# Causal attention on one core: fp32r pieces with two heads in 64-row tiles, row maxima folded per 512 queries in a stream ahead of the scores, PV two steps behind

## What is computed

```python
def attn(x, W_qkv, b_qkv, W_proj, b_proj):          # H = 16, HS = 16
    q, k, v = split(heads(x @ W_qkv + b_qkv))
    q, k = rope(q), rope(k)
    att = einsum('bhqd,bhkd->bhqk', q, k) / sqrt(HS)
    att = softmax(where(causal, att, -1e9), axis=-1)
    return merge(einsum('bhqk,bhkd->bhqd', att, v)) @ W_proj + b_proj
x = layernorm(x + attn(x))
x = layernorm(x + moe_ffn(x))
```

## Time and profile before

| | |
|---|---|
| median of three runs | 1558.74 us |
| profiled execution | 1565.56 us |
| its span | 1563.8 us |
| PE busy, share of the span | 1339.1 us, 86% |
| DVE | 1167.3 us, 75% |
| ACT | 799.7 us, 51% |
| POOL | 276.2 us, 18% |
| DMA moved | 126.96 MB, mean 81 GB/s |

### The profile page before, as it was taken

How to read it: one execution, slowest core, us unless ns; L and a number is a source line. 1 busy time by engine, 2 the same in 40 slices (tenths; PEclk the granted TensorE clock), 3 DMA queues, 4 the chain that set the end, 5 groups by cost and what they waited for, 6 DMA issues and landing times. The chain is left out here.

```text
span 1563.8 us, 26808 instructions
## 1 busy us (share of the span) xinstructions
PE 1339.1 (86%) x7840; PEld 655.1 (42%) x7840; DVE 1167.3 (75%) x2833; ACT 799.7 (51%) x1130; POOL 276.2 (18%) x282
## 2 busy tenths in 40 slices
PE   6766299899999998998998998999947765999997
PEld 3433111233333233332332332332236655999997
DVE  6997499898897797986996896880036754888886
ACT  3443100366665565665665665668825443545452
POOL 3554500001001001011001001011123331121112
PEclk9887555799999999999998999999978876999999
DMA  4587592001201201102112113000045623333420
GB/s 163 174 192 228 155 140 36 2 29 29 82 29 54 58 29 56 55 28 79 33 50 79 29 37 83 8 9 14 14 149 167 214 78 98 101 100 114 137 95 23
DMA packets 117980, 126.96 MB, mean 81 GB/s; under 512 B 14428, under 2 KB 100447, under 8 KB 117856
## 3 DMA queue, kind: packets, MB, share of 16 engines
q1 hardware_dynamic: 114272, 116.97, 26.4%
q0 software_dynamic: 3584, 8.47, 1.5%
HBM read 82.98 MB, written 48.38 MB: 84 GB/s over the span
## 5 line engine op out<-in xcount | busy, mean ns | idle before, releaser
L622 ACT ACTIVATE probs<-scores 128x1024 f32<-128x1024 f32 (+3 forms) x640 | 540.7, 895 | 415.7 <-PE scores L524 414.8
L669 DVE TENSOR_REDUCE part_max<-ring 128x1 f32<-128x512 f32 x768 | 484.5, 685 | 34.1 <-PE ring L552 32.2
L552 PE MATMUL ring<-k_stack,q_stack 96*128 96x512 bf16 (+3 forms) x1280 | 433.8, 383 | 64.7 <-DMA k_stack<-pieces_d 29.9
L524 PE MATMUL scores<-q_stack,k_stack 99*128 99x512 bf16 (+3 forms) x1280 | 344.1, 358 | 12.4 <-ACT probs L622 6.3
L542 PE MATMUL out_p<-probs,v_s 128*32 128x512 f32 (+3 forms) x2560 | 306.9, 552 | 9.3 <-POOL probs L714 5.5
L664 DVE CUSTOM_DVE_ANT_0 scratch<-ring,mask_s 128x384 f32<-128x384 f32 (+3 forms) x512 | 229.6, 488 | 100.9 <-issue 88.2
L552 PEld LDWEIGHTS ring<-k_stack,q_stack 96*128 96x128 bf16 x1280 | 120.5, 99 | 418.0 <-DVE part_max L669 170.3
L714 POOL TENSOR_SCALAR_AFFINE_SELECT probs<-probs 128x512 f32<-128x512 f32 x128 | 81.2, 634 | 865.6 <-ACT probs L622 865.6
L524 PEld LDWEIGHTS scores<-q_stack,k_stack 99*128 99x128 bf16 x1280 | 114.0, 100 | 169.9 <-ACT probs L622 67.6
L195 PE MATMUL psP<-xT,wqk_s 128*128 128x512 f32 x128 | 72.4, 731 | 34.5 <-ACT xT L234 30.7
L542 PEld LDWEIGHTS out_p<-probs,v_s 128*32 128x32 f32 x2560 | 51.6, 109 | 112.4 <-issue 90.5
(11 more groups left out here) (116 smaller groups left out, 1455.6 us busy)
## 6 DMA issues: line engine op xcount, KB each, us to landing
w_whole<-w SPq DMA_DIRECT2D x16, 1024.0 KB, 6.3
q_stack<-pieces_d SPq DMA_DIRECT2D x192, 64.0 KB, 2.7
k_stack<-pieces_d SPq DMA_DIRECT2D x192, 64.0 KB, 2.8
v_d<-vt SPq DMA_DIRECT2D x8, 1024.0 KB, 4.4
v_s<-v_d SPq DMA_DIRECT2D x8, 1024.0 KB, 6.0
o_d<-o_s SPq DMA_DIRECT2D x32, 256.0 KB, 2.1
p_o<-o_d SPq DMA_DIRECT2D x8, 1024.0 KB, 6.0
slots_d<-no_row SPq DMA_DIRECT2D x1, 5200.0 KB, 30.3
```

The costliest lines, as they stand in the source:

```text
L524: last = nc.tensor.matmul(scores[p][:, hh, off:CHUNK], k_stack[i][0:KROWS, j, kb * P:(kb + 1) * P], q_stack[i][0:KROWS, j, c * CHUNK + off ...
L552: nc.tensor.matmul(ring[m % 3][:, 0:w], q_stack[i][0:SROWS, j, qt * P:(qt + 1) * P], k_stack[i][0:SROWS, j, t * CHUNK:t * CHUNK + w], star ...
L622: nc.scalar.activation(probs[n % 2][:, 2 * p:2 * p + 2, off:CHUNK], scores[p][:, :, off:CHUNK], ACT.Exp, scale=SCALE).then_inc(exp_done[p], 1)
L669: nc.vector.tensor_reduce(out, ring[m % 3][:, 0:w], axis=AX.X, op=ALU.max).then_inc(ring_read, 1)
```

## The change

- **Pieces.** `TERMS` has three products instead of six, over two pieces (`hi`, `low`) of type fp32r (stored as 4 bytes). `rest`, `cut_mid` and the tile `mid` are gone; `low` is raw minus hi on GpSimd. A stack is 48 rows and 2 rows of the maximum: 50 rows, so one head lies in rows 0 to 63 and another in rows 64 to 127.
- **Scores.** The two matmuls of a pair p use the two halves of the rows. Each writes its own PSUM bank.
- **Maxima.** 144 blocks per unit (`ITEMS`): a full block is one head, 48 rows; diagonal blocks of 128 and 256 columns hold two heads of one row half. In each diagonal block TensorE adds the causal mask by a further bf16 matmul of 128 columns (identity times mask) to each head, and VectorE always uses `tensor_reduce`. The blocks go by chunk of queries, and there are three folds per unit (chunk 3, chunk 2, chunks 1 and 0), each with its transpose, its cut (`cut_maxima`) and 4 DMAs (`load_max`). The stream runs 74 items (`LEAD`) ahead of the scores and on over the units without a break; only these 74 are done ahead of the first score.
- **PV** lags two steps (`LAG`), `probs` has four buffers, and the PV of a step is issued in two halves of 256 columns, one behind each pair of scores.
- The rows of ones come by DMA instead of a memset on GpSimd; unit 1's stacks are loaded after the first maxima.

```diff
-TERMS = [(0, 0), (0, 1), (1, 0), (1, 1), (0, 2), (2, 0)]
+TERMS = [(0, 0), (0, 1), (1, 0)]
...
-NPIECE = 3
+NPIECE = 2
...
-        hi = [sb(f"hi{i}", [P, QKG, CHUNK], BF16) for i in range(2)]
-        mid = [sb(f"mid{i}", [P, QKG, CHUNK], BF16) for i in range(2)]
-        low = [sb(f"low{i}", [P, QKG, CHUNK], BF16) for i in range(2)]
+        hi = [sb(f"hi{i}", [P, QKG, CHUNK], F32R) for i in range(2)]
+        low = [sb(f"low{i}", [P, QKG, CHUNK], F32R) for i in range(2)]
...
-            def cut_mid(b, c, g):
-                i, n = c % 2, NCH * b + c
-                act.wait_ge(rest_ready, QKG * n + g + 1)
-                nc.scalar.activation(mid[i][:, g, :], rots[i][:, g, :], ACT.Copy).then_inc(mid_ready, 1)
...
+NPROB = 4
+LAG = 2
+def max_items():
+    items, fold_after, turn_at = [], {}, {}
+    for c in ORDER:
+        block = []
+        for t in range(c, -1, -1):
+            for qt in range(TPC * c, TPC * (c + 1)):
+                w = (qt + 1) * P - t * CHUNK if t == c else CHUNK
+                if 2 * w <= CHUNK:
+                    block += [(qt, t, half, 2, w, True) for half in range(2)]
+                else:
+                    block += [(qt, t, j, 1, w, t == c) for j in range(HPU)]
+        before = {NCH - 1: 2, NCH - 2: 0, NCH - 3: 1}.get(c)
+        if before is not None:
+            block.insert(3, before)
+            turn_at[before] = len(items) + 3
+        items += block
...
+LEAD = TURN_AT[0] + 10
...
+            def score_pair(u, i, n, p):
+                c, kb, off = STEPS[n]
+                pe.wait_ge(exp_done[p], NSTEP * u + n)
+                for hh in range(2):
+                    rows = slice(hh * HALF, hh * HALF + KROWS)
+                    last = nc.tensor.matmul(scores[p][:, hh, off:CHUNK],
+                                            k_stack[i][rows, kb // TPC, p, kb % TPC * P:(kb % TPC + 1) * P],
+                                            q_stack[i][rows, c, p, off:CHUNK],
+                                            start=True, stop=True)
+                last.then_inc(scores_ready[p], 1)
...
+            def max_item(u, i, m, uses):
+                qt, t, j, heads, w, diag = ITEMS[m]
...
+                    pe.wait_ge(ring_read, NRING * u + m - 2)
+                slot = ring[m % 3][:, 0:heads * w]
+                for h in range(heads):
+                    rows = slice(j % 2 * HALF, j % 2 * HALF + SROWS)
+                    pair = j // 2 if heads == 1 else h
+                    last = nc.tensor.matmul(slot[:, h * w:(h + 1) * w], ...
+                                            start=True, stop=not diag)
+                    if diag:
+                        last = nc.tensor.matmul(slot[:, h * w + w - P:(h + 1) * w], id16[:], mask_s[:],
+                                                start=False, stop=True)
+                last.then_inc(ring_full, 1)
...
+            def step(u, i, uses, n, ahead, behind):
+                first, stop = PLAN[n]
+                middle = (first + stop) // 2
+                chunk_waits(u, n)
+                score_pair(u, i, n, 0)
+                items(u, i, uses, first, middle, ahead)
+                if behind:
+                    pv_waits(*behind[0:1], behind[2])
+                    pv_cols(behind[1], behind[2], FIRST_COLS)
+                score_pair(u, i, n, 1)
+                items(u, i, uses, middle, stop, ahead)
+                if behind:
+                    pv_cols(behind[1], behind[2], LAST_COLS)
...
             def read_max(u, m):
-                    nc.vector.tensor_tensor_reduce(out=scratch[:, j, 0:w], in0=ring[m % 3][:, 0:w],
-                                                   in1=mask_s[:, CHUNK - w:CHUNK], scale=1.0, scalar=LOWEST,
-                                                   op0=ALU.add, op1=ALU.max, accum_out=out).then_inc(ring_read, 1)
...
+                    nc.vector.tensor_reduce(part_max[:, qt, j:HPU:2, t],
+                                            ring[m % 3][:, 0:heads * w].rearrange("p (h w) -> p h w", h=heads),
+                                            axis=AX.X, op=ALU.max).then_inc(ring_read, 1)
```

More of the change, by code:

```diff
@@ L382, in max_plan @@
+ITEMS, FOLD_AFTER, TURN_AT = max_items()
+NRING = len(ITEMS)
+FOLDS = [(NCH - 1,), (NCH - 2,), tuple(range(NCH - 3, -1, -1))]
+FOLD_OF = [2, 2, 1, 0]
+NMAXROW = [HPU * TPC * len(f) for f in FOLDS]
+assert NRING % 3 == 0
+LEAD = TURN_AT[0] + 10
+def max_plan():
+    cost = [0.6 if isinstance(item, int) else 0.08 + item[3] * item[4] / 960 for item in ITEMS]
+    width = [CHUNK - off for _, _, off in STEPS]
+    plan, m, seen, done = [], LEAD, 0, 0.0
+    for w in width:
         seen += w
         start = m
-        while m < NMAX and sum(jobs[:m + 1]) - early <= seen / total * (sum(jobs) - early) + 1e-6:
+        while m < LEAD + NRING and done + cost[m % NRING] <= seen / sum(width) * sum(cost) + 1e-6:
+            done += cost[m % NRING]
@@ L385, in max_plan, with attention @@
             m += 1
-        plan[n] = range(start, m)
-    assert m == NMAX
+        plan.append((start, m))
+    assert m == LEAD + NRING
     return plan
 PLAN = max_plan()
[L393 to L398, removed]
+def attention(nc, pieces_d, v_d, causal16, ident, ident16, o_d):
@@ L476, in store_o, with unit @@
                 sp.dma_start(o_d[NCH * b + c, g], o_s[c % 2][:]).then_inc(o_stored[c % 2], 16)
[L478 to L483, removed]
+            def unit(u, b, g, i, last, two_ahead):
+                load_max(1, i, NRING * u + TURN_AT[1] + 1)
+                store_o(u, b, g, 3)
+                if two_ahead:
+                    load_chunk(two_ahead[0], two_ahead[1], i, 3)
+                load_max(2, i, NRING * (u + 1) + (1 if last else TURN_AT[2] + 1))
+                store_o(u, b, g, 2)
+                if two_ahead:
+                    load_chunk(two_ahead[0], two_ahead[1], i, 2)
+                if not last:
+                    load_max(0, 1 - i, NRING * (u + 1) + TURN_AT[0] + 1)
+                for c in (1, 0):
@@ new lines, in max_item, with turn_maxima, maxima @@
+                last.then_inc(ring_full, 1)
+            def turn_maxima(f, u, m):
+                pe.wait_ge(folded[f], u + 1)
+                pe.wait_ge(ring_read, NRING * u + m - 2)
+                nc.tensor.transpose(ring[m % 3][0:NMAXROW[f], 0:P], row_max[f][:], id_s[:]).then_inc(ring_full, 1)
+            def maxima(u, i, uses, first, stop):
+                for m in range(first, stop):
+                    if isinstance(ITEMS[m], int):
+                        turn_maxima(ITEMS[m], u, m)
+                    else:
+                        max_item(u, i, m, uses)
@@ new lines, in items, with chunk_waits @@
+            def items(u, i, uses, first, stop, ahead):
+                maxima(u, i, uses[0], min(first, NRING), min(stop, NRING))
+                if stop <= NRING:
+                    return
+                if ahead:
+                    maxima(u + 1, 1 - i, uses[1], max(first, NRING) - NRING, max(stop, NRING) - NRING)
+                elif first <= NRING:
+                    turn_maxima(2, u + 1, 0)
+            def chunk_waits(u, n):
+                c, kb, _ = STEPS[n]
+                if kb == 0 and c != 0:
+                    f = FOLD_OF[c]
+                    pe.wait_ge(max_loaded[f], MAX_PRIMED[f] + MAX_DMAS * (u + 1))
```

365 lines of the change are left out of this document (163 added, 202 removed).

## The result

The change makes the kernel slower: 2035.6 us (median of four runs, 2018.47 to 2037.93) against 1558.58 (four runs), a ratio of 1.304, 95% interval 1.3004 to 1.3077. The forecast was 1462, its range ended at 1570, and the slower rival stood at 1597.

What follows compares the result with a forecast made beforehand. PE was taken to bound the units, DVE close behind. Projection 10, lead 44 and units 42 us made 96 off the profiled 1565.6 us: 1470, or 1462 against the median; range 1365 to 1570.

Steps and rivals of the forecast that it cites:

- the slower rival: Scores: fp32r matmuls of two row halves run one behind the other, 121 us a unit, 1597 us in all; chance 0.13.
- Projection: Projection groups: one DVE operation and ACT's `mid` go, more is stored; 10 us off, between 20 off and 5 on.
- Lead: Before the first score: DVE does 74 items instead of 160 blocks; 52 us instead of 96, 44 off.
- DVE, 89 a unit: DVE's work in a unit: 64 us for full blocks and folds, 25 for diagonal ones, 89 in all.
- Pairs side by side: Scores on PE: two heads' matmuls overlap, 0.22 us and a little a pair, 17 us a unit instead of 30.
- The second rival: Scores: matmuls of two row halves do not overlap, PE has 13 us more a unit, 1597 us; chance 0.13.
- Full blocks: Maxima on PE: 96 full blocks a unit at 0.22 us each, 21 us.
- PV bursts: PV on PE: 72 bursts a unit instead of 40, each 0.27 us over streaming; PV is 48 us a unit.
- Masks: Diagonal blocks on PE: 64 mask matmuls a unit at 0.15 us each, 10 us a unit (3.5 to 21).
- The upper bound in the prediction: Units with masks at 0.33 us and, as stated, no pairs: 116 us a unit, 1560 us in all.
- Waits: Units: later PV takes GpSimd's mask and ACT's exp off PE's path; DVE's 2.88 us idle at the fold is covered.
- Sum: Whole kernel: units at 103 us take 42 off; with projection and lead 96 off, 1462 us against the median.

Runs made afterwards that it cites:

- e7: Kernel before the change, with its score and maxima matmuls over rows 0 to 49 only (results wrong): 2131.33 us.
- e5: Changed kernel with masks left out (maxima over too many keys) and PV in one burst of 512 columns: 1544.63 us.
- e1: Changed kernel with scores and maxima in 128-row tiles, two heads' rows summed per matmul (scores wrong): 1744.8 us.
- e9: Stacks, pieces and projection of the kernel before, order of the changed kernel, PV in two bursts of 256 columns: 1578.96 us.
- e8: Stacks, pieces and projection of the kernel before, order of the changed kernel, PV in one burst: 1550.77 us, ratio 0.993 to the kernel before.
- e4: Changed kernel with scores and maxima reading the upper 16 bits of stack elements as bf16, same 64-row tiles: 1615.4 us.

## Why the prediction was wrong

**The step that failed** is the one that costs every matmul of the units at the high clock: "It streams at 0.21 per 128 columns", "a pair takes 0.22 and a little", taken from a kernel whose stacks had 96 and 99 rows. The prediction named the clock only for the lead, and none of its rivals was about it. The two sizes above, 2.16 and 1.23 us for the same half step, are what was missed. The profile had a warning: ahead of the first score PE was busy 81.63 of 85 us at 1.2 GHz, so a busy PE did not assure the high clock; that rows were a part of it, no row of before could tell. In its place the runs show: in the kernel before, fewer rows alone take the units from 0.97 to 0.50 (e7); in the changed kernel, 48 or 50 rows a matmul together with masks and extra bursts do it, for taking those two out brings the clock over the span from 0.655 to 0.858 (e5), and filling the rows brings it to 0.883 (e1). The Trainium skill, "TensorE: Matmul & The Clock Gate", Part 1: The HAM clock gate, says that a monitor of how busy the engine has been sets the clock. By that rule a TensorE busy 174.90 of 175 us has the high clock; the trace has 0.61.

**Point by point.**
- *Projection*: 18 us instead of 10, inside its bounds.
- *Lead*: 54 against 52, right, low clock included.
- *DVE, 89 a unit*: it is busy 96.35 and 89.23 of 175 us, some 89 in a unit's 167. It never became the bound over a unit, since PE was.
- *Pairs side by side*: right. At the high clock 0.33 behind a PV and 0.24 in a row; "0.22 and a little" was too low for the first. The second rival, tiles one behind the other, is refuted.
- *Full blocks*: 0.22 each was too much. Two of them run side by side as well, 0.33 for both (905.17 to 905.50), some 5 us a unit less; the pairs of scores at 0.33 take about as much back.
- *PV bursts*: 906.07 - 905.50 = 0.57 for 256 columns, 0.14 over streaming, as put (the entry, 0.12 in the forecast, comes on top). In e9 a further burst cost 0.11.
- *Masks*: 0.15 was wrong; 0.36, the upper bound of 0.33 and a little. The Trainium skill, "TensorEngine Tiling (Array Packing)", Key Properties, says that a change of tiling mode drains the engine, and the trace agrees between 64 and 128 rows: 0.36 against 0.06 in tall tiles. I had it before me and took less. At the high clock that alone is 64 x 0.2 = 13 us a unit, some 100 in all: the forecast would have been about 1560, no gain. The upper bound in the prediction, 1560 "at 0.33 and no pairs", is in truth the sum with pairs; without them it is 76 + 53 = 129 a unit, some 1655, so the range was too narrow by its own terms.
- *Waits*: right for this kernel. PE is idle 11 us in all from 227.6 to 1615. But it was slow enough for nothing to hold it; with the high clock e8 shows the hole at the fold.
- *Sum*: measured and forecast lie 2036 - 1462 = 574 us apart. The masks' size is about 100 of them by that estimate. The rest, some 470, I put down to the clock; that share is an estimate, since no run had this kernel at the high clock throughout. The trace bears it out roughly: with each distance between two matmul starts replaced by the mean one of the same two kinds at the high clock (and left as it is where there is none), the seven units from 227.6 take 827 us and not 1171, 118 a unit where the forecast with masks at 0.36 gives 116.

Direction and size were both wrong, and the range too: it was made of bounds of terms that all assumed one clock. The terms that came out right (lead, pairs, bursts) did not help, as all were small beside it.

## What to carry to other kernels

Splitting the array's rows halves the time of two matmuls only if the clock survives it: before taking a cost from a kernel with taller stacks, count how many rows hold data at a time, and what stands between the matmuls, not only how long TensorE is busy. Bring work that is far from full (small masks, narrow steps, extra bursts) into the same tile as its neighbours; in tall tiles a mask cost 0.02 us, between half tiles 0.36 and some of the clock with it. Without masks and second bursts the half tiles came to 1544.63 us (with the maxima taken over too many keys), 1% under the kernel before. The order (a stream of maxima ahead, PV later) and the layout (64-row fp32r) should be tried apart: with PV in one burst the order gave 0.7%, with two bursts it cost 1.2%, and the layout on top of that cost 29% (1578.96 to 2036).

## What was not expected of the hardware

- The kernel before, with its scores and maxima over 50, 64 or 66 rows instead of 96 and 99 and nothing else changed, goes from 1561 to 2131, 2045 and 2081 us, the granted clock over the span from 0.90 to 0.62, 0.65 and 0.64.
- Busy time tells nothing of it: PE is busy 174.90 of 175 us at a mean of 0.61.
- Short rows do not bar the high clock by themselves: pairs of 64-row tiles without masks and with PV whole have 0.86 over the attention part (e5).
- The same half step takes 2.16 us at the low clock and 1.23 at the high one, and in e4 the clock went from 1.00 to 0.50 within 40 us as masks and narrow steps came.
- At the high clock fp32r pairs in two row halves follow each other at 0.24 us per pair of 512 columns, weight loads included.
